# Half of the last three chunks' mask bytes turned by VectorE instead of TensorE, with their loads split over two DMA queues

## The reference

```
h = max(layernorm(x), 0);  Wh = h @ W
e[i, j] = leaky_relu(Wh[i] @ a1 + Wh[j] @ a2, slope 0.2)
attention = softmax(where(adj > 0, e, -9e15), axis=1)
out = x + elu(attention @ Wh)
```

## Time and profile before

| | |
|---|---|
| Median of 3 runs | 245.09 us (244.29 to 245.14) |
| The profiled execution | 244.79 us, of which the trace spans 243.0 |
| PE (TensorE) busy | 227.0 us, 93% of the span |
| DVE (VectorE) busy | 196.4 us, 81% |
| ACT (ScalarE) busy | 156.2 us, 64% |
| POOL (GpSimd) busy | 59.1 us, 24% |

### The profile page before, as it was taken

The page is one execution under the profiler, slowest core; times in us unless marked ns, Lnnn a source line. Parts: engine busy times, 40 slices in busy tenths (PEclk is TensorE's granted clock), DMA queues, the critical chain, the costliest instruction groups (busy, mean ns, idle before and its releaser), DMA issues.

```text
span 243.0 us, 8254 instructions
## 1 busy us (share of the span) xinstructions
PE 227.0 (93%) x3736; PEld 221.2 (91%) x3736; DVE 196.4 (81%) x259; ACT 156.2 (64%) x139; POOL 59.1 (24%) x48
## 2 busy tenths in 40 slices
PE   6969999599999999999999999999999999999970
PEld 2759899599998999999999999999999999999970
DVE  4999997536776998889887988898879888998864
ACT  3698836697799999944996677019975774000051
POOL 3648036897000070300000560000001710040000
PEclk9997999999999999999999999999999999999995
DMA  6999999999998999999999999999999300020002
GB/s 225 360 389 386 386 386 385 388 367 370 301 352 284 363 395 386 388 385 385 398 386 385 388 385 385 385 387 369 386 386 386 140 0 3 3 89 3 3 0 92
DMA packets 36521, 71.92 MB, mean 296 GB/s; under 512 B 1282, under 2 KB 1924, under 8 KB 36484
## 3 DMA queue, kind: packets, MB, share of 16 engines
q1 hardware_dynamic: 35520, 69.74, 79.0%
...
## 4 chain that ended last, share of the span: by engine, by line
PE 74%; ACT 8%; DVE 7%; issue 4%; POOL 4%; DMA 1%; ACTq 0%; DVEq 0%; POOLq 0%
PE acc L834 20%; PE acc L835 20%; PE acc L836 20%; PE mask_t L817 11%; ACT mask L420 4%; POOL v L330 2%; POOL val L333 2%; ACT neg L432 1%; DVE words L610 1%; DVE stats L547 1%; DMA x_sb<-in_x_dram 1%; PE acc L796 1%; PE acc L805 1%; ACT neg L511 1%; DVE wh_sb L573 1%
## 5 line engine op out<-in xcount | busy, mean ns | idle before, releaser
L610 DVE SCALAR_TENSOR_TENSOR words<-g_row,gq_word,mask_t 128x1024 f32<-128x1024 f32 x128 | 161.4, 1278 | 36.0 <-PE acc L836 19.0
L834 PE MATMUL acc<-val,words 128*128 128x129 f16 x1000 | 171.9, 220 | 0.3 <-DVE wh_sb L573 0.3
L835 PE MATMUL acc<-val,words 128*128 128x129 f16 x1000 | 171.9, 220 | 0.0
L836 PE MATMUL acc<-val,words 128*128 128x129 f16 x1000 | 171.9, 220 | 0.0
L420 ACT ACTIVATE mask<-raw,step_bias 128x2048 uint8<-128x2048 int32 x63 | 121.8, 1993 | 28.4 <-DVE x_sb L626 17.3
L834 PEld LDWEIGHTS acc<-val,words 128*128 128x128 f16 x1000 | 97.8, 98 | 0.5 <-issue 0.5
L835 PEld LDWEIGHTS acc<-val,words 128*128 128x128 f16 x1000 | 97.9, 98 | 0.1
L836 PEld LDWEIGHTS acc<-val,words 128*128 128x128 f16 x1000 | 97.8, 98 | 0.0
L817 PE MATMUL mask_t<-ident_b,mask 128*128 128x128 bf16 x512 | 34.3, 221 | 1.8 <-ACT mask L420 1.8
L817 PEld LDWEIGHTS mask_t<-ident_b,mask 128*128 128x128 bf16 x512 | 30.3, 99 | 2.2 <-ACT mask L420 2.2
L358 POOL TENSOR_TENSOR hp<-num,rz 128x1024 f32<-128x1024 f32 x3 | 5.7, 1897 | 105.3 <-DVE rz L621 105.3
...
## 6 DMA issues: line engine op xcount, KB each, us to landing
...
a_sb<-in_L_gnn_a_dram ACTq DMA_DIRECT2D x1, 1.0 KB
```

Source lines behind the costliest of these rows:

```text
L610: nc.vector.scalar_tensor_tensor(words[:, q], g_row[:, c * CHUNK:(c + 1) * CHUNK], gq_word[:, 1, t:t + 1], maskt_bytes[:, u % 2, q // 2, : ...
L834: nc.tensor.matmul(acc_tile(t), high, val[:, tile, 0, 0:V], start=first and t % PT == 0, stop=False, skip_group_check=True)
L835: nc.tensor.matmul(acc_tile(t), high, val[:, tile, 1, 0:V], start=False, stop=False, skip_group_check=True)
L836: last = nc.tensor.matmul(acc_tile(t), low, val[:, tile, 0, 0:V], start=False, stop=False, skip_group_check=True)
```

## The change

Columns 2048 to 4095 (units 4 to 7) of chunks 1 to 3 are no longer turned by TensorE. They are taken as a **set**: the 1024 x 2048 block of a chunk, read in four loads h = 0 to 3. Load h brings 256 rows, laid out so that partition 32k + r holds the columns of unit 4 + k. Each is four DMAs of 32 partitions (512 KB each): SP issues those to partitions 0 to 63, ACT those to partitions 64 to 127. ACT writes bytes into three pair buffers of two units each (two of them in memory of `h_t` and `v32`, one in slots 2 and 3 of `mask`), and DVE turns each unit with one instruction over 32 x 32 squares of four-byte groups (`turn_set`), issued ahead of the last word of the unit before. The column numbers and values of these units are needed in the matching layout; POOL moves them once with 16 copies of 32 x 640 words (`move_values`).

With it come other moves. `mask` has two slots for turned units from chunk 1 on. Chunks 2 and 3 run their units in the order 4, 5, 0, 6, 1, 7, 2, 3; chunk 1 keeps 0 to 7. The loads are numbered by `LOADS`: 0 to 7 are chunk 0, 8 to 11 units 0 to 3 of chunk 1, 12 to 15 its set, 16 to 19 the set of chunk 2, 20 to 23 its units 0 to 3, 24 to 27 the set of chunk 3, 28 to 31 its units 0 to 3. ACT issues its halves in the two runs 12 to 19 and 24 to 27. The sum of the squares leaves its place ahead of chunk 1 and goes behind loads 14 to 17. DVE's `result` becomes a third POOL pass, and ACT's part of `tail` follows load 13, load 22 and load 31. The rows of x for chunks 1 to 3 are loaded a second time (1.5 MB), and the last store is three DMAs in place of four.

The new tables, and how SP issues the loads:

```diff
+    SETS = C - 3
+    ORDER = [[*range(U)] if c <= SETS else [4, 5, 0, 6, 1, 7, 2, 3] for c in range(C)]
+
+    LOADS = [(c, u, None) for c in range(SETS) for u in range(U)]
+    LOADS += [(SETS, u, None) for u in range(4)] + [(c, None, h) for c in (SETS, SETS + 1) for h in range(4)]
+    LOADS += [(SETS + 1, u, None) for u in range(4)] + [(SETS + 2, None, h) for h in range(4)] + [(SETS + 2, u, None) for u in range(4)]
+    RUNS = ((12, 20), (24, 28))
+
...
+        def is_set(c, u):
+            return c >= SETS and u >= 4
+
+        def turning(c, u):
+
+            if c < SETS:
+                return c * U + u + 1, c * U + u + 1 - RING
+            i = SETS * U + (c - SETS) * 4 + u
+            return i + 1, i + 1 - (RING if i < SETS * U + 2 else 2)
+
+        def mask_slot(c, u):
+            return u % RING if c < SETS else u % 2
...
-            for n in range(1, C * U):
-                for k in range(2):
-
-                    if n == RING and k == 0:
-                        sp.wait_ge(first_bytes, 1)
-                    elif n >= RING:
-                        sp.wait_ge(act_bytes, 2 * (n - RING) + k)
-                    load_raw(n, k)
+            for at in range(1, C * U):
+
+                if LOADS[at][1] is None:
+                    sp.wait_ge(act_bytes, 2 * (at - RING) + 1)
+                    load_set(at)
+                else:
+                    for k in range(2):
+                        if (at, k) == (RING, 0):
+                            sp.wait_ge(first_bytes, 1)
+                        elif at >= RING:
+                            sp.wait_ge(act_bytes, 2 * (at - RING) + (1 if LOADS[at - RING][1] is None else k))
+                        load_raw(at, k)
+                if at == U:
+
+                    sp.wait_ge(ht_ps, NB)
+                    load_rows(SETS)
+                if at == 26:
+
+                    sp.wait_ge(words_free, U * BT)
+                    sp.wait_ge(val_moved, MOVES)
+                    sp.wait_ge(squares_ready, G)
+                    load_rows(C - 2)
+                    load_rows(C - 1)
+
+            last = out_lin[C - 1].rearrange("p (t f) -> p t f", f=F)
+            for k, (t0, t1) in enumerate(BANKS):
+                sp.wait_ge(last_res, k + 1)
+                sp.dma_start(last[:, t0:t1], rows_of(C - 1)[:, t0:t1]).then_inc(out_done, 16)
```

POOL, ACT, DVE and TensorE:

```diff
-                pool.wait_ge(hp_ready, c + 2)
-                pool.nop(nofuse=True)
-                nc.gpsimd.tensor_scalar(neg[:], hp[:], 0.0, None, ALU.min).then_inc(neg_ready, 1)
+
+                pool.wait_ge(neg_ready, c + 1)
+                nc.gpsimd.tensor_scalar(hp[:], hp[:], 0.0, -1.0, ALU.max, ALU.add).then_inc(pos_ready, 1)
                 pool.wait_ge(pos_ready, c + 1)
-                nc.gpsimd.tensor_tensor(hp[:], hp[:], x_sb[:, group(c)], ALU.add).then_inc(sum_ready, 1)
+                if c >= SETS:
+                    pool.wait_ge(rows_in[c], 16)
+                nc.gpsimd.tensor_tensor(hp[:], hp[:], rows_of(c), ALU.add).then_inc(sum_ready, 1)
+                pool.wait_ge(sum_ready, c + 1)
+                pool.wait_ge(ex_ready, c + 1)
+                nc.gpsimd.tensor_tensor(rows_of(c), hp[:], neg[:], ALU.add).then_inc(res_ready, 1)
                 pool.wait_ge(res_ready, c + 1)
...
+            def move_values():
+
+                pool.wait_ge(vl_ready, G - 1)
+                pool.wait_ge(pad_ready, 2)
+
+                pool.wait_ge(ht_ps, NB)
+                moves = 0
+                for k in range(4):
+                    for m in range(4):
+
+                        if moves:
+                            pool.wait_ge(val_moved, moves)
+                        moves += 1
+                        nc.gpsimd.tensor_copy(val_set_u[k * QUARTER:(k + 1) * QUARTER, 4 * m:4 * m + 4],
+                                              val_u[m * QUARTER:(m + 1) * QUARTER, (4 + k) * BT:(5 + k) * BT]).then_inc(val_moved, 1)
+                pool.wait_ge(val_moved, MOVES)
+
+            move_values()
+            tail(0)
...
+            def set_to_bytes(c, h):
+
+                at = LOADS.index((c, None, h))
+                act.wait_ge(set_in[at % RING], 64 * FILLED[at])
+                for k in range(2):
+                    if c == SETS:
+
+                        act.wait_ge(mean_ps, 1)
+                        act.wait_ge(wh_ps, 3 * G)
+                    elif (c, k) == (SETS + 1, 0):
+
+                        act.wait_ge(turned, SETS * U)
+                    else:
+
+                        act.wait_ge(set_turned, 4 * (c - SETS) + 2 * k - 4)
+                    nc.scalar.activation(pair_bytes[PAIRS[c][k]][:, :, h],
+                                         raw[:, at % RING, :, k * 256:(k + 1) * 256].rearrange("p t (m x) -> p m t x", m=2), ACT.Sign,
+                                         scale=1.0, bias=step_bias[:, 0:1]).then_inc(act_bytes, 1)
+
+            def load_set(at):
+
+                c, _, h = LOADS[at]
+                act.wait_ge(act_bytes, 2 * (at - RING) + 1)
+                for k in ACT_QUARTERS:
+                    act.dma_start(raw[k * QUARTER:(k + 1) * QUARTER, at % RING], adj_set[c, 1, h, k]).then_inc(set_in[at % RING], 16)
+
+            def load_sets(at):
+
+                for a0, a1 in RUNS:
+                    if at == a0 - 2:
+                        act.wait_ge(raw_in[(a0 - 1) % RING][0], FILLED[a0 - 1] * 16)
+                        for a in range(a0, a0 + 3):
+                            load_set(a)
+                    elif a0 + 3 <= at + RING < a1:
+                        load_set(at + RING)
...
-            act.wait_ge(vh_ready, 2 + G - 1)
-            for g in range(G):
-                square(g)
 
             def tail(c):
-
+                act.wait_ge(hp_ready, c + 2)
+                nc.scalar.activation(neg[:], hp[:], ACT.Relu, scale=-1.0).then_inc(neg_ready, 1)
                 act.wait_ge(neg_ready, c + 1)
-                nc.scalar.activation(hp[:], hp[:], ACT.Relu).then_inc(pos_ready, 1)
-                nc.scalar.activation(neg[:], neg[:], ACT.Exp).then_inc(ex_ready, 1)
+                nc.scalar.activation(neg[:], neg[:], ACT.Exp, scale=-1.0).then_inc(ex_ready, 1)
...
+            for at in range(U, C * U):
+                c, u, h = LOADS[at]
+                if u is None:
+                    set_to_bytes(c, h)
+                else:
                     for k in range(2):
                         to_bytes(c, u, k)
-                tail(c - 1)
-                for u in range(6, U):
-                    for k in range(2):
-                        to_bytes(c, u, k)
-                store(c - 1)
+                load_sets(at)
+                if at == 13:
+                    tail(0)
+                if 14 <= at < 14 + G:
+                    square(at - 14)
+                if at == 15:
+                    store(0)
+                if at == 22:
+                    tail(1)
+                if at == 26:
+                    store(1)
+            tail(2)
+            store(2)
...
+            def turn_set(c, i):
+
+                m = ORDER[c][i] - 4
+                if m == 0:
+                    dve.wait_ge(act_bytes, 2 * LOADS.index((c, None, 3)) + 1)
+
+                dve.wait_ge(words_ready, 4 * (c * U + i - 1))
+                nc.vector.transpose(maskt_quads[:, i % 2].rearrange("p (t h r) -> p t h r", h=4, r=QUARTER),
+                                    pair_quads[PAIRS[c][m // 2]][:, m % 2]).then_inc(set_turned, 1)
...
+                if is_set(c, u):
+                    word, bytes_t = word_set[:, t - T // 2, 0, V // 2 + 1:V // 2 + 2], maskt_fourths[:, i % 2, q]
+                else:
+                    word, bytes_t = gq_word[:, 1, t:t + 1], maskt_bytes[:, i % 2, q // 2, :, q % 2]
+                nc.vector.scalar_tensor_tensor(words[:, q], g_row[:, c * CHUNK:(c + 1) * CHUNK], word, bytes_t, ALU.max, ALU.mult
+                                               ).then_inc(words_ready, 1)
...
+                        if q == BT - 1 and u < U - 1 and is_set(c, ORDER[c][u + 1]):
+                            turn_set(c, u + 1)
+                        if (u, q) == (U - 1, BT - 1) and c < C - 1 and is_set(c + 1, ORDER[c + 1][0]):
+                            turn_set(c + 1, 0)
                         weights(c, u, q)
                         if (u, q) == (0, 2):
                             take_sums(c - 1)
-                        if (u, q) == (4, 3):
-                            result(c - 1)
...
+            def turn_ahead(c, i):
+
+                if i == U - 1:
+                    c, i = c + 1, -1
+                if not is_set(c, ORDER[c][i + 1]):
+                    turn(c, i + 1)
```

174 lines of the change are left out of this document (111 added, 63 removed).

## The result

The changed kernel takes 264.3 us (median of four runs, 263.16 to 265.26) against 245.06 for the kernel before in the same runs: ratio 1.079, 95% interval 1.0735 to 1.0848. It is slower by 19 us, far above the range of the prediction. Its profiled execution took 263.6 us; the sum above gave 244.5 for that, so 19.1 us are to be found.

What follows compares the result with a forecast made beforehand. TensorE's work was taken as the bound: its end at 235.44 us, minus 10.7 and 0.4, plus stops of 10.5 and 0.9, gave 235.6, and 244.8 for the runs' median; range for 8 in 10: 240.5 to 251.5.

Steps and rivals of the forecast that it cites:

- the sum above: Whole kernel: TensorE's end at 235.6 us plus the end of the run, 244.5 us for the profiled execution.
- TensorE saves 12 x 0.89, its second turn comes at 83.6, it stops at 106.7: TensorE: 12 of 32 unit turns leave it, 10.7 us; chunk 1's second turn at 83.63; it stops at 106.7.
- Its data are there: Load 15 in chunk 1's set: issued at 88.5 to 89.3, landed before ACT asks at 106.2; bytes at 110.0.
- near 180: Load 27, in chunk 3's set: bytes near 180 us, against 182 when wanted.
- ACT's issues: ACT ahead of load 15: 0.40 us an issue, 0.8 a load, four pairs 3.2 us.
- The two mask slots: ACT in chunk 1: load 10 may start only at 78.3 us, load 11 at 84.7, after turns end.
- 385 GB/s without a pause until slice 31: DMA before the change: full at 385 GB/s, but ending 45 us ahead of TensorE.
- DVE's pace, the square turn at 1.19, chunk 2's first product 30.2 us behind load 15: DVE from load 15's bytes: 25 turns and words at 1.19 us plus 0.45; chunk 2's first product at 140.3.
- That rival: Dear DVE turn: at 2.4 us each, 252 us in all; together with slower ACT bytes in set form, chance 0.24.
- I count nothing: TensorE's clock after the stop 106.7 to 112.4: two products at half rate, 2.7 us, inside 4.8 spare.
- Edits at no cost: POOL's 16 copies at 1.9 us end at 89.7; third POOL pass in idle time; x's 1.5 MB 4 us, under 45 spare.
- halves of partitions do not add up: Set loads from two queues: 10.9 us a load, not 5.4; 293 us; decides from 6.5 a load; chance 0.10.

Runs made afterwards that it cites:

- own buffer: Third pair buffer in wh_sb's memory, so `mask` keeps four slots: on the changed kernel 257.4 us (one run); with sets in chunks 2 and 3 only, 250.4 us.
- the sets of chunks 2 and 3 apart: Sets in chunks 2 and 3 only, each behind its chunk's plain units, four mask slots: 265.0 us with ACT issuing behind each load, 257.3 with both queues entering together.
- two edits: On the changed kernel, one run each: third pair buffer outside `mask`, 257.4 us; ACT issuing its halves behind each load that frees a slot, 259.5 us.
- all three edits: Changed kernel with third pair buffer outside `mask`, ACT issuing behind each load, and tail and squares later: 263.6 us (one run).

## Why the prediction was wrong, step by step

- *TensorE saves 12 x 0.89, its second turn comes at 83.6, it stops at 106.7*: right (106.69).
- *"Its data are there"*: the step that failed, and by most. It took the earlier trace rows, a landing of 1 MB over whole partitions with the queue at 385 GB/s, for a load in another form. In halves the stream ran at 203 to 367. In the sum ACT was to start on load 13 at 93.9 (84.7, two loads of 3.8 and two pairs of 0.8); the data of load 12 held it until 94.7 and those of load 13 until 100.3. That is 6.4 us, before anything that ACT's later issues add. Load 15 came 9.4 us late, and load 27 was bytes at 199.6 against *"near 180"*. With the same issues but whole partitions, the first square turn came at 111.6, not 119.4.
- *ACT's issues: "0.40 us" each, "so 0.8 for its share of a load"*: too small as well. The row was for stores that had ACT's queue to themselves. Four pairs took 4.3 us with whole partitions and 9.2 in halves, where 3.2 stood in the sum; a pair of halves took 1.48 to 3.64, and six in a row 6 to 7.5. Against whole partitions from SP alone, ACT's issues delay the first square turn by 5.2 us, so by 2 more than the sum had.
- *The two mask slots*: the waits ahead of loads 10 and 11 were in the sum as time of ACT, and were right as that. What was not in it is that ACT's first halves wait with load 10 while SP's are issued from 73.3 on and run alone (203 GB/s from 78 to 84). With a buffer of its own ACT's halves are issued 3.6 us earlier and load 11 starts 3.1 us earlier; the first square turn comes 6.9 us earlier, and that is as much as the end gains (7). At load 22 the wait of 6.9 us has the same effect (207), but an own buffer brings chunk 3's first square turn only 4.5 us forward, so no further gain shows there.
- *DMA at "385 GB/s without a pause until slice 31"*: a misreading of the earlier trace rows, which has 367 down to 284 in slices 9 to 14. Nothing in the sum hangs on it.
- *DVE's pace, the square turn at 1.19, chunk 2's first product 30.2 us behind load 15*: right (turns of 1.25 us, the next instruction 1.16 behind; 30.2 measured). The estimate from the Trainium skill, VectorE: DVE Perf Modes, "The three transpose paths", of 2.5 us was twice too high. That rival is out.
- *Clock: "I count nothing"*: right in chunk 1, where the clock was 0.50 until 127 us but DVE set the pace. Chunk 3 began behind a stop that the sum did not have: from 206 to 212 us the clock was 0.69 and TensorE did 73 matmuls, where a stretch of 6 us at 1.00 has 110, and the chunk took 1.6 us longer than forecast.
- *Edits at no cost*: POOL's 16 copies took 12.4 us (0.77 each), all hidden. The end, with three stores, took 8.4 us against 8.9 in the sum; where the other half microsecond went was not looked at.
- *The rival "halves of partitions do not add up"* had the right place and 0.10. Its bound was too crude (10.9 us a load if they serialize, or 5.4); they add up in part. At 298 to 367 GB/s a load of 2.1 MB is 5.7 to 7.0 us, just about the 6.5 from which it was to decide; in the stretches where one side ran alone, at 203 to 207, it would be 10. So the rival that was nearest to the cause had the smallest chance, and its own time, 293, was far off too.

What stays open: why plain loads slow down beside halves, when early issues on ACT help (they saved 5 us in the changed kernel, and cost 8 with the sets of chunks 2 and 3 apart), why the second run of set loads stays slow when both queues have issued, and why the saving of two edits was lost there when they were joined; no run took those apart. The kernels with the own buffer, with whole partitions from both queues and with all three edits ran once each, so differences of a microsecond between them are not to be leant on.
